# A two-layer transformer decoder on one core: X loaded in four pieces, the projections read X in place, the output stored block by block in the last stage

## What is computed

```python
x = layernorm(x + attention0(x))            # rotary, 16 heads of 16, causal
x = layernorm(x + cross_attention0(x, ctx))
x = layernorm(x + mixture_of_experts0(x))
x = layernorm(x + differential_attention1(x))  # 32 half heads of 8, rotary
x = layernorm(x + latent_attention1(ctx, x))
x = layernorm(x + expert_choice1(x))
# both attentions begin with
q, k, v = x @ Wq.T, x @ Wk.T, x @ Wv.T      # q and k are then rotated
```

## Time and profile before

| | us |
|---|---|
| median of 3 runs | 4306.84 (4303.91 to 4312.91) |
| the profiled execution | 4314.04 |
| its span in the profile | 4312.3 |
| PE, VectorE, ACT, POOL busy in it | 3587.0, 2920.0, 1941.5, 733.0 |
| DMA, mean over the span | 44 GB/s |

### The profile page before, as it was taken

One profiled execution on the slowest core, in us unless ns is written; L12 is line 12 of the kernel. 1 busy time (PEld: TensorE's weight loads), 2 busy tenths in 40 slices (PEclk: granted clock), 3 DMA queues, 4 the chain that ended last, 5 costly groups with the idle time before them and its releaser, 6 DMA issues. The chain is left out here.

```text
span 4312.3 us, 64417 instructions
## 1 busy us (share of the span) xinstructions
PE 3587.0 (83%) x19064; PEld 1729.3 (40%) x19064; DVE 2920.0 (68%) x4353; ACT 1941.5 (45%) x3763; POOL 733.0 (17%) x1015
## 2 busy tenths in 40 slices
PE   7599999576398778999999999999756699998857
PEld 4244443443244343333333333333233354544625
DVE  6576674456455579898888888898365377774275
ACT  2166665133101134777777777777612223332121
POOL 3222222033200050000000000000014324443000
PEclk9599898788699887999999999999977799997578
DMA  5311110200000150000000000000111321000202
GB/s 200 107 46 46 45 45 16 76 20 5 30 10 15 52 187 20 17 24 17 17 24 17 21 20 17 24 16 17 18 32 68 111 68 42 25 18 28 97 16 72
DMA packets 133312, 187.95 MB, mean 44 GB/s; under 512 B 71881, under 2 KB 89170, under 8 KB 131634
## 3 DMA queue, kind: packets, MB, share of 16 engines
q1 hardware_dynamic: 132178, 178.21, 14.1%
q10 hardware_dynamic: 864, 6.29, 0.4%
HBM read 87.63 MB, written 54.72 MB: 33 GB/s over the span
## 5 line engine op out<-in xcount | busy, mean ns | idle before, releaser
L631 DVE TENSOR_REDUCE L_attn_tops<-L_attn_psM 128x2 f32<-128x1024 f32 (+3 forms) x1408 | 1559.7, 1147 | 323.2 <-PE L_attn_psM L741 314.6
L568 ACT ACTIVATE L_attn_E<-L_attn_psS 128x512 f32<-128x512 f32 (+3 forms) x2816 | 1388.6, 576 | 570.1 <-PE L_attn_psS L700 566.6
L700 PE MATMUL L_attn_psS<-L_attn_Q,L_attn_K 64*128 64x512 f32 (+3 forms) x2816 | 992.9, 436 | 108.1 <-ACT L_attn_E L568 38.3
L741 PE MATMUL L_attn_psM<-L_attn_K,L_attn_Q 62*128 62x512 f32 (+3 forms) x2816 | 1017.1, 480 | 57.3 <-DMA L_attn_K<-parts_k 30.2
L700 PEld LDWEIGHTS L_attn_psS<-L_attn_Q,L_attn_K 64*128 64x128 f32 x2816 | 471.3, 191 | 801.5 <-ACT L_attn_E L568 639.0
L716 PE MATMUL L_attn_psO<-L_attn_E,L_attn_V 128*32 128x512 f32 (+3 forms) x5632 | 732.9, 594 | 0.0
L741 PEld LDWEIGHTS L_attn_psM<-L_attn_K,L_attn_Q 62*128 62x128 f32 x2816 | 431.6, 193 | 170.0 <-DVE L_attn_tops L631 54.5
L526 POOL TENSOR_TENSOR L_AO<-L_attn_o 128x128 f32 (+1 forms) x64 | 29.3, 458 | 1460.6 <-DVE L_attn_o L664 1460.6
L1418 PE MATMUL m_psE<-m_we,m_xT 128*128 128x512 f32 x512 | 237.6, 624 | 0.0
L535 POOL TENSOR_SCALAR_AFFINE_SELECT L_attn_E<-L_attn_E 128x128 f32<-128x128 f32 x512 | 146.2, 292 | 448.1 <-ACT L_attn_E L568 436.8
L2108 ACT ACTIVATE x_E<-x_psS 128x512 f32<-128x512 f32 x256 | 138.9, 595 | 181.7 <-PE x_psS L2231 179.6
(11 more groups left out here) (341 smaller groups left out, 3865.8 us busy)
## 6 DMA issues: line engine op xcount, KB each, us to landing
parts_q<-L_proj_parts SPq DMA_DIRECT2D x64, 256.0 KB
parts_k<-L_proj_parts SPq DMA_DIRECT2D x64, 256.0 KB
L_attn_Q<-parts_q SPq DMA_DIRECT2D x192, 64.0 KB
L_attn_K<-parts_k SPq DMA_DIRECT2D x192, 64.0 KB
L_attn_Q<-parts_q SPq DMA_DIRECT2D x64, 128.0 KB
L_attn_K<-parts_k SPq DMA_DIRECT2D x64, 128.0 KB
L_merge_h<-L_AO SPq DMA_DIRECT2D x64, 128.0 KB, 2.4
queries<-x1p_qo SPq DMA_DIRECT2D x16, 512.0 KB
```

What stands on the lines that cost most here:

```text
L568: act.activation(E[(4 * n + s) % 8][:, c0:], psS[bank][:, c0:], ACT.Exp, scale=scale).then_inc(e_done, 1)
L631: dve.tensor_reduce(dst, src, AX, ALU.max).then_inc(m_read, 1)
L700: pe.matmul(psS[bank][:, c0:], K[g.slot][r:r + RH, c, kt * P:(kt + 1) * P], Q[g.slot][r:r + RH, c, q * HALF + c0:(q + 1) * HALF], start=Tr ...
L741: last = pe.matmul(psM[bank][:, j * HALF:j * HALF + n], Q[t.slot][r:r + TOP, c, qt * P:(qt + 1) * P], K[t.slot][r:r + TOP, c, h * HALF:h * ...
```

## The change

- `load_start`: the identity is loaded first, X in four DMAs of 1 MB, one per batch block, each with a semaphore of its own (`x_in`); VectorE waits for the identity alone, so the block can end with X still on its way.
- `project`: no `xs` buffers and no copies into them. PE's transposes read X itself; in layer 0 the first transposes of each block wait for that block's `x_in`. PE's wait for the weights moves behind the first four units of transposes. All loops over the two passes are written out, and the transposes and copies for a block that doesn't exist are left out.
- `take`: ACT's loop of eight is written out; after the square root of block i it waits for block i - 1's last write to X and issues that block's store of 512 KB on its own queue; the last block's store follows after the loop, and ACT waits for all eight. `store` is gone.

```diff
--- before.py
+++ after.py
@@ -125,15 +125,18 @@
 
     X, ident, identb = keep["X"], keep["ident"], keep["identb"]
     loaded = sems.sem("start_loaded")
+    keep["x_in"] = [sems.sem(f"start_x_in{b}") for b in range(B)]
     with nc.Block() as block:
         @block.sync
         def _(sp):
-            sp.dma_start(X[:], a["x"].rearrange("(t p) d -> p t d", p=P)).then_inc(loaded, 16)
             sp.dma_start(ident[:], a["ident"]).then_inc(loaded, 16)
+            for b in range(B):
+                sp.dma_start(X[:, b * TB:(b + 1) * TB, :], a["x"].rearrange("(t p) d -> p t d", p=P)[:, b * TB:(b + 1) * TB, :])\
+                    .then_inc(keep["x_in"][b], 16)
 
         @block.vector
         def _(dve):
-            dve.wait_ge(loaded, 32)
+            dve.wait_ge(loaded, 16)
             dve.tensor_copy(identb[:], ident[:])
 
 
@@ -150,7 +153,6 @@
     PT = keep["PT"]
     with ExitStack() as ctx:
         m = Mem(nc, ctx)
-        xs = [m.sb(f"{tag}_proj_xs{k}", [P, TB, D]) for k in range(2)]
         xt = [m.sb(f"{tag}_proj_xt{k}", [P, DC, S]) for k in range(2)]
         wqk = m.sb(f"{tag}_proj_wqk", [P, DC, 2 * D])
         wv = m.sb(f"{tag}_proj_wv", [P, DC, D])
@@ -164,7 +166,7 @@
         psQ = [m.ps(f"{tag}_proj_psQ{k}", HALF) for k in range(2)]
         psV = [m.ps(f"{tag}_proj_psV{k}", HALF) for k in range(2)]
         weights = sems.sem(f"{tag}_proj_weights")
-        xs_in = [sems.sem(f"{tag}_proj_xs_in{k}") for k in range(2)]
+        x_in = keep["x_in"] if tag == "L0" else None
         turned = sems.sem(f"{tag}_proj_turned")
         xt_in = sems.sem(f"{tag}_proj_xt_in")
         qk_done = sems.sem(f"{tag}_proj_qk_done")
@@ -181,14 +183,11 @@
         with nc.Block() as block:
             @block.sync
             def _(sp):
-                for k in range(2):
-                    sp.dma_start(xs[k][:], X[:, k * TB:(k + 1) * TB, :]).then_inc(xs_in[k], 16)
-                    if k == 0:
-                        sp.dma_start(wqk[:], a[f"{tag}_wqk"]).then_inc(weights, 16)
-                        sp.dma_start(wv[:], a[f"{tag}_wv"]).then_inc(weights, 16)
-                        sp.dma_start(cos[:], a[f"{tag}_cos"]).then_inc(weights, 16)
-                        sp.dma_start(sin[:], a[f"{tag}_sin"]).then_inc(weights, 16)
-                with sp.Fori(0, B // 2) as i:
+                sp.dma_start(wqk[:], a[f"{tag}_wqk"]).then_inc(weights, 16)
+                sp.dma_start(wv[:], a[f"{tag}_wv"]).then_inc(weights, 16)
+                sp.dma_start(cos[:], a[f"{tag}_cos"]).then_inc(weights, 16)
+                sp.dma_start(sin[:], a[f"{tag}_sin"]).then_inc(weights, 16)
+                for i in range(B // 2):
                     for u in range(N // 2):
                         k, qk, c = u // 4, u % 4 // 2, u % 2
 
@@ -200,12 +199,10 @@
                                              parts[u % 4][64 * h:64 * h + 64, p, :].bitcast(F32)).then_inc(out[u % 4], 16)
                 for k in range(4):
                     sp.wait_ge(out[k], OUT * (N // 8) * (B // 2))
-                sp.wait_ge(xs_in[0], 32)
-                sp.wait_ge(xs_in[1], 48)
 
             @block.gpsimd
             def _(pool):
-                with pool.Fori(0, B // 2) as i:
+                for i in range(B // 2):
                     for n in range(N):
 
                         pool.wait_ge(qk_read, i * (3 * N) + 6 + 3 * (n + 1))
@@ -233,15 +230,12 @@
                 for u in range(4):
                     xt_copy(0, 0, u, 0)
 
-                act.dma_start(xs[0][:], X[:, 2 * TB:3 * TB, :]).then_inc(xs_in[0], 16)
-                with act.Fori(0, B // 2) as i:
+                for i in range(B // 2):
                     for n in range(N):
                         k, j = n // PERB, n % PERB // 2
                         if n % 2 == 0:
-                            xt_copy(i, 1 - k, j, 4 + 4 * k)
-                            if n == 6:
-
-                                act.dma_start(xs[1][:], X[:, 3 * TB:4 * TB, :]).then_inc(xs_in[1], 16)
+                            if 2 * i + k + 1 < B:
+                                xt_copy(i, 1 - k, j, 4 + 4 * k)
                         else:
                             act.wait_ge(v_done, i * 8 + 4 * k + j + 1)
                             src = psV[j % 2][:].rearrange("p (t g w) -> p g t w", t=2, g=gb)
@@ -272,7 +266,7 @@
                     to, col = parts[n // 2 % 4], slice((n % 2) * HALF, (n % 2 + 1) * HALF)
                     dve.tensor_tensor(to[:, 1, col], rot[n % 4][:], to[:, 0, col].bitcast(F32), ALU.subtract).then_inc(low, 1)
 
-                with dve.Fori(0, B // 2) as i:
+                for i in range(B // 2):
                     for n in range(N + 2):
                         if n < N:
                             rotate(i, n)
@@ -281,30 +275,26 @@
 
             @block.tensor
             def _(pe):
-                pe.wait_ge(weights, 64)
-
-                def transposes(i, k, u, turns):
+                def transposes(b, k, i, u, turns):
                     c, h = u // 2, u % 2
+                    if u == 0 and x_in is not None:
+                        pe.wait_ge(x_in[b], 16)
 
                     pe.wait_ge(xt_in, i * 8 + turns + u + 1)
                     for t in range(4):
-                        last = pe.transpose(psT[u % 2][:, t * P:(t + 1) * P], xs[k][:, 4 * h + t, c * P:(c + 1) * P], ident[:])
+                        last = pe.transpose(psT[u % 2][:, t * P:(t + 1) * P], X[:, b * TB + 4 * h + t, c * P:(c + 1) * P], ident[:])
                     last.then_inc(turned, 1)
 
-                pe.wait_ge(xs_in[0], 16)
                 for u in range(4):
-                    transposes(0, 0, u, 0)
-                with pe.Fori(0, B // 2) as i:
+                    transposes(0, 0, 0, u, 0)
+                pe.wait_ge(weights, 64)
+                for i in range(B // 2):
                     for n in range(N):
                         k, unit = n // PERB, n % PERB
                         g, h, j = unit // 2, unit % 2, unit // 2
                         if unit == 0:
 
                             pe.wait_ge(xt_in, i * 8 + 4 * k + 6)
-                            if k == 0:
-                                pe.wait_ge(xs_in[1], i * 16 + 16)
-                            else:
-                                pe.wait_ge(xs_in[0], 32)
 
                         pe.wait_ge(qk_read, i * (3 * N) + 3 * n + 3)
                         for c in range(DC):
@@ -312,7 +302,8 @@
                                              xt[k][:, c, h * HALF:(h + 1) * HALF], start=(c == 0), stop=(c == DC - 1))
                         last.then_inc(qk_done, 1)
                         if h == 0:
-                            transposes(i, 1 - k, j, 4 + 4 * k)
+                            if 2 * i + k + 1 < B:
+                                transposes(2 * i + k + 1, 1 - k, i, j, 4 + 4 * k)
                         else:
                             pe.wait_ge(v_read, i * 8 + 4 * k + j + 1)
                             for t in range(2):
@@ -2559,6 +2550,7 @@
         n_dve = sem("n_dve")
         n_act = sem("n_act")
         passed = sem("passed")
+        stored = sem("stored")
         with nc.Block() as block:
             @block.sync
             def _(sp):
@@ -2603,9 +2595,19 @@
             @block.scalar
             def _(act):
                 act.wait_ge(const, 1)
-                with act.Fori(0, NB) as i:
+
+                def put(i):
+                    act.wait_ge(n_dve, i * 5 + 5)
+                    act.dma_start(a["y"].rearrange("(t p) d -> p t d", p=P)[:, i * BLK:(i + 1) * BLK, :],
+                                  X[:, i * BLK:(i + 1) * BLK, :]).then_inc(stored, 16)
+
+                for i in range(NB):
                     act.wait_ge(n_dve, i * 5 + 3)
                     act.activation(sd[:], mv[:, :, 1], ACT.Sqrt, bias=eps[:]).then_inc(n_act, 1)
+                    if i:
+                        put(i - 1)
+                put(NB - 1)
+                act.wait_ge(stored, 16 * NB)
 
             @block.vector
             def _(dve):
@@ -2644,15 +2646,6 @@
                 run_turns(dve, turn, NB, 1, 2, 2)
 
 
-def store(nc, a, keep, sems):
-    out = sems.sem("stored")
-    with nc.Block() as block:
-        @block.sync
-        def _(sp):
-            sp.dma_start(a["y"].rearrange("(t p) d -> p t d", p=P), keep["X"][:]).then_inc(out, 16)
-            sp.wait_ge(out, 16)
-
-
 def attention(nc, a, keep, sems, layer, dh, groups):
 
     with nc.cleanup_on_exit(), ExitStack() as own:
@@ -2716,7 +2709,6 @@
                                      ("A1", attention, (1, 8, 32)), ("X1", latent_attention, ()), ("F1", expert_choice, ())):
             if stages is None or name in stages:
                 sublayer(nc, a, keep, sems, *args)
-        store(nc, a, keep, sems)
 
 
 def layouts(x):
```

## The result

The changed kernel takes 4288.82 us (median of 22 executions, 4272.37 to 4308.50), the kernel before beside it 4319.42 (22 executions, 4303.91 to 4342.15): ratio 0.993, interval 0.9915 to 0.9945, or 30 us less (24 to 37). The forecast was 4277.7 (4267 to 4288) and a saving of 29.1.

What follows compares the result with a forecast made beforehand. VectorE was taken to bound the first projection and PE the last stage, with the change touching only idle ends. Terms 9.3 + 3.8 + 5.5 + 10.5 = 29.1 us off the 4306.84 median gave 4277.7 us, range 4267 to 4288.

Steps and rivals of the forecast that it cites:

- the base: Whole kernel: the 4306.84 us median of the runs shown, from which the saving was subtracted unchanged.
- Start: Kernel start: weights stream right behind X, first matmul at 20.7 in place of 31.47; gain 9.3 us (7.0 to 10.8).
- The term of 1.5 for the clock: Kernel start: idling between transposes and matmuls may put half clock on real work; cost 1.5 us (0 to 3.8).
- X in place, layer 0: First projection's tail: without the 1 MB copies' traffic the stores keep up better; gain 3.8 us (0 to 9.2).
- rival A: Late layer 0 stores slow by themselves (0), both starts cold (7.0 and 4.7), end 10.5: 22.2 us saved; chance 0.15.
- Start of layer 1: Second projection's start: no copy ahead of the weights, transposes no longer wait; gain 5.5 us (4.2 to 7.9).
- Loops written out: Both projections: written-out loops and dropped last transposes gain 0, at most 1.1 us per projection.
- End: Kernel end: seven of eight output stores go out while PE works; gain 10.5 us (9.5 to 11.4).
- the term for the copies: First projection's tail: the 3.8 us gain forecast from removing the copies of X that hold back stores.
- B: Clock kept at both starts (10.8 and 7.9), first projection's tail 8, end 11: 37.7 us saved; chance 0.11.
- C: Load and output stores: pieces run on fewer DMA engines, weights land at about 28; 18.3 us saved; chance 0.08.
- D: Written-out second passes: instructions arrive late, net 12.5 us slower; chance 0.02, and 0.02 in part (no change).

Runs made afterwards that it cites:

- e6: The changed kernel run again with no edit: 4275.56 us against 4328.58 for the kernel before, ratio 0.9893.
- e2: The kernel before with only the end changed (block stores on ScalarE's queue): one time, 4320.81 us beside 4320.63 for the kernel before.
- e3: The changed kernel with one 1 MB copy of X per pass put back, into a buffer nobody reads: 4286.35 us, one execution.
- e5: The changed kernel with X loaded as one DMA and still read in place; profiled span 4270.0 us.
- e11: The changed kernel with X loaded as one DMA and still read in place, timed: 4289.22 us against 4322.13 for the kernel before, ratio 0.9926.
- e10: The kernel before with only the projections' loops written out: 4327.07 us against 4322.13, ratio 1.0013.
- e9: The kernel before with only the end changed (block stores on ScalarE's queue), timed: 4311.85 us against 4322.13, ratio 0.9977.
- e7: The changed kernel with layer 0's weights issued behind X's first piece, ahead of the other three: 4281.80 us, ratio 0.9902 to the kernel before.
- e8: As e7, with layer 1's projection weights also loaded during the experts stage into own buffers: 4264.16 us, ratio 0.9873 to the kernel before.

## Why the forecast was right in the saving and wrong in the time

*The step that failed* is the base: "The median of the runs shown is 4306.84, which is 7.2 lower; I carry the saving over unchanged." Three executions don't fix a median here. Of 55 further executions of the kernel before, in this and the later comparisons, one lies at or below 4306.84; their median is 4323.4 and they run from 4299 to 4342. Against the 4319.42 of the first comparison the same saving gives 4290.3, 1.5 from the measured 4288.82. And the range, 21 us wide, was built from the terms of the saving alone; the base was given no width, though three executions already differed by 9.

*Start*: 9.3 forecast (7.0 to 10.8), 10.3 measured. The first matmul came at 21.3, I had 20.7. The term of 1.5 for the clock was nothing: the half clock lay on the first unit only, as it had before (in e6 the second unit took 2.62 us in place of 1.88, so it can cost a little). My ground for that term was weak: e2 shows that the clock of the first unit changes from one execution of the same code to the next.

*X in place, layer 0*: 3.8 forecast, 2.1 between the two traces; over the traces, tails without the change's start are 14.9 to 19.3 (mean 17.1), those of the changed kernel, e3, e5 and e11 13.7 to 15.3 (mean 14.7). The 14.3 lies between the 12 to 13 that would have shown the term right and rival A's 16. The mechanism is there but small. Its premise, that the stores run at 207 GB/s whenever no copy runs, does not hold: 166 in the changed kernel and 175 to 205 in the kernel before, with VectorE at its end and no copy beside them. I had read one stretch of the first pass. What the copies cost is nearer 1 us (e3).

*Start of layer 1*: 5.5 forecast (4.2 to 7.9), 7.1 measured. First matmul 7.7 us after the write instead of 16.3 (8 to 9 said); the half clock took 1.4 us on the first unit and nothing on the second, where I had allowed 2.4.

*Loops written out*: 0 forecast; 0 within the noise by e10 (rotations 93.5 to 93.1, ratio 1.0013). The Trainium skill (Runtime: NRT & Kernel Launch, Instruction fetch mechanics) prefers unrolling, since a taken branch out of the fetched pages stalls; the border of the passes is 3.21 us with the loop and 3.20 without it, so nothing of that can be seen here.

*End*: 10.5 forecast, 10.8 in the profile, 10.3 between e9's medians (3 to 17 by the interval). A store of 512 KB lands after 3.0 us (median of eight; 3.1 said), and ACT was idle for 8.6 to 10.1 us before each square root but the first.

Sum: 29.1 forecast; 31.0 in the touched parts, 30 (24 to 37) timed. That the sum is so near is partly luck: the term for the copies was 1.7 too high, the two starts and the end 2.9 too low together, and 0.7 of the rotations and layer 1's tail is in no term.

*Rivals.* A (22.2) is out by its cold starts, and its word on the late stores is mostly right. (It prices the second start at 4.7, where the term's own lower bound is 4.2.) B (37.7) is out by the tail. C is out: the pieces came in at a DMA share of 1.10 and 353 GB/s, with the weights at 21.3 and not 28, and the stores of the output landed in 3.0 us (median). The Trainium skill's rule (DMA: Bandwidth & Descriptors, on why a DMA increments by 16), that the slowest dimension gives the number of DMA engines, up to 16, agrees: 128 here, and a share of 0.48 to 0.51 for stores in 8 groups. D is out by e10's rotations.

## What to carry to other kernels

At a border of stages, ask what the last wait is made of: here some 26 of 31 us came from taking a 1 MB copy and the transposes out of the weights' way and from storing results while the last stage still computes, and some 12 more lie in issuing the weights earlier still. A producer that starts earlier gains only as far as the queue behind it keeps up: in its one trace, e7 had 4 of its 10 us back as a longer wait for stores, e8 1.5. And a forecast of a time needs a base with a width: measure the kernel before more than three times, and forecast the saving and the base apart.

## What the runs showed of the hardware that was not expected

- The same program differs by 36 and 38 us (0.8 and 0.9%) between the 22 executions of either kernel in the first comparison, and its time goes with the mean granted clock: the changed kernel's execution at 0.880 took 4308.5 us, those at 0.889 took 4272.4 and 4279.2. In layer 0's attention alone it is 36 us (603.0 at a mean clock of 0.89, 639.0 at 0.83), in which half-clock stretches follow short stops of PE; the same kind of stop doesn't always bring one.
- Stores of 4 KB rows at one DMA share (0.49 to 0.52) bring 166 to 205 GB/s with VectorE at its end and no engine feeding them. What sets that was not tried.
- The clock of the first matmuls after a stop is not a property of the code: the same four, behind the same 0.86 us of idling, took 3.78 us in the kernel before and 1.98 in e2.
